# Two-layer block, layer 1's experts: weighted rows added to the outcome in DRAM by an indirect transfer

## The chip, the cores and the metric

One Trainium2 chip, one core of it. The metric is the device time of one execution in microseconds, the median of several runs. 512 tokens (two sequences) of 512 floats pass through two layers; all tensors are float32.

## The reference, cut to what is computed

Each of the two layers adds three parts to x: a cross-attention, a second mixing part (linear attention in layer 0, an mLSTM in layer 1) and a mixture of experts. The last one, layer 1's, is what the change touches:

```python
logits = xf @ gate_w + gate_b
scores = jax.nn.softmax(logits.astype(jnp.float32), axis=-1)
top_vals, top_idx = jax.lax.top_k(scores, TOPK)             # 2 of 16
cw = (jax.nn.one_hot(top_idx, N_EXPERTS) * weights[..., None]).sum(axis=1)
h = jnp.einsum('td,edh->teh', xf, w1) + b1                  # 512 -> 704
g = jnp.einsum('td,edh->teh', xf, w3) + b3
a = jax.nn.silu(h) * g
y = jnp.einsum('teh,ehd,te->td', a, w2, cw) + cw @ b2       # 704 -> 512
z = jax.nn.silu(xf @ sw1 + sb1) * (xf @ sw3 + sb3) @ sw2 + sb2
return (y + z).reshape(shape)
```

So the outcome is x plus the shared expert's z, plus for each token the rows that its two experts give, times their gates, plus the gates times b2.

## The kernel before, in words

The program is one stream per engine, written out stage by stage; engines meet at counting semaphores. x stays in SBUF as `x_tok`, 128 partitions by 4 tiles of tokens by 512. TensorE (PE) multiplies, VectorE (DVE) and ScalarE (ACT) take results out of PSUM, GpSimd (POOL) does some vector work and all indirect DMAs, SyncE (SP) issues the weight loads.

Both layers' experts share a class, `Experts`. Its steps, in the order of the work:

- `route_vector` takes softmax and the top experts per token. `place_tensor` (L1588) counts with triangular matmuls which place each token has in its expert's list, and `place_vector` (L1609 to L1631) works out from that the slot in the list (`slot`, 512 slots per expert), the place of a token's row in the experts' output (`first_at`, and `rest_at` for places from 128 on), the gate for either (`first_gate`, `rest_gate`), and whether any expert has over 128 tokens (`over`).
- `place_gpsimd` (L1643) scatters token numbers into a list in DRAM, one indirect DMA per tile of tokens and choice: 12 in layer 0, 8 in layer 1, 128 words each. The lists are cleared at the program's start (L878). `list_sync` (L1666) loads the list, `list_vector` casts it (L1673), `list_tensor` turns it (L1680), DVE copies it out again (L1675).
- `gather_rows` (L1686) fetches 128 token rows of 2 KB for an expert from `token_rows`, a copy of the normalized x in DRAM, in four buffers that rotate. `turn_rows` (L1714) transposes them, `rows_vector` (L1721) copies them out.
- Per expert of layer 1 PE makes 96 products with w1 and w3 (L242), turns the next expert's rows, and then makes the 18 products of the down projection of the expert before (L1757 to L1759, three per tile since w2 and the hidden rows are split in a high and a low part). ACT: six Silu (L2824), six casts of w2 (L1733), and the copy of the finished 128x512 bank to one of three buffers (L1766), which ACT then stores to `expert_out` in DRAM (L1768). The copy waits until the store before from the same buffer has landed.
- After the last expert POOL waits for all stores and gathers the rows back per tile of tokens and choice (L1795, 8 gathers in layer 1), DVE adds each, times its gate, to x (L1807), and SP stores a tile of x as soon as it is complete (L2868, `store_sync`, 4 stores of 256 KB).

The order around the change: in `experts1_sync` SP issues 48 weight loads of 1.4 MB, three per expert, into eight slots; load 8 waits for expert 0's up products, later ones for up or down products of an expert (L2629 on). In `experts1_vector` DVE adds the shared expert's three groups of products (L2745) and the bias products (L1660) to x before the first routed expert; the third group comes after the list. In `experts1_gpsimd` POOL adds `sb2` to x, scatters, issues three gathers, then the others as PE's turns free their buffers, and then the gathers back. A branch (`if_over`) holds a second form of the whole for experts with over 128 tokens; with these inputs it is not entered. At the start POOL makes the constants (L260 to L282) and SP, after its first loads, issues the clears of the two lists (L878).

Of the kernel before, what the change touches and what calls it, by code (L numbers as in the profile page):

```python
# [6 lines left out]
P = 128  # L7
F32 = mybir.dt.float32
F32R = mybir.dt.float32r
I32 = mybir.dt.int32  # L10
# [71 lines left out]
def build_program(nc, A, out_dram):  # L82
# [40 lines left out]
    HID0_AT, DOWN1_AT, HID1 = SPLIT_ARENA + 2 * SLOT, 11712, HT1 * P  # L123
# [13 lines left out]
    zero_words = sbuf("zero_words", [E0 * CHUNKS, P], I32)  # L137
    norm_small = sbuf("norm_small", [P, 2, NT, 10])
    square = sbuf("square", [P, DIM])

    token_rows = nc.dram_tensor("token_rows", (TOK, DIM), F32, kind="Internal").ap()
    ids, expert_out, expert_rest = {}, {}, {}
    for layer, n in ((0, E0), (1, E1)):
        ids[layer] = nc.dram_tensor(f"ids{layer}", (n * CAP, 1), I32, kind="Internal").ap()
        expert_out[layer] = nc.dram_tensor(f"expert_out{layer}", (n * P, DIM), F32, kind="Internal").ap()
        expert_rest[layer] = nc.dram_tensor(f"expert_rest{layer}", (n * (CAP - P), DIM), F32, kind="Internal").ap()
# [107 lines left out]
    IDENT, MASKS, TRI, NUMBERS, TOKEN_NO, ZERO_WORDS = 1, 2, 3, 4, 5, 6  # L254
# [4 lines left out]
    def constants_gpsimd(pool):  # L259
# [22 lines left out]
        pool.memset(zero_words[:, :], 0).then_inc(consts, 1)  # L282

# [581 lines left out]
    def cross0_sync(sp):  # L865
# [10 lines left out]
        sp.wait_ge(consts, ZERO_WORDS)  # L876
        for layer, n in ((0, E0), (1, E1)):
            sp.dma_start(ids[layer].rearrange("(c p) o -> c (p o)", p=P),  # L878
                         zero_words[0:n * CHUNKS, :]).then_inc(cleared[layer], 16)
# [601 lines left out]
    class Experts:  # L1481

        def __init__(self, layer, n, chosen, hidden_tiles, last_first, L, S, before=None):
# [10 lines left out]
            self.rank, self.is_first, self.base, self.at_f = (S(NT, chosen) for _ in range(4))  # L1494
            self.first_at, self.rest_at = (S(NT, chosen).bitcast(I32) for _ in range(2))
            self.first_gate, self.rest_gate = (S(NT, chosen) for _ in range(2))
# [3 lines left out]
            self.ids_row, self.ids = L(P), L(P)  # L1500
            self.gather = [arena[:, ARENA - (i + 1) * DIM:ARENA - i * DIM] for i in range(4)]

            self.totals = {"routed": 1, "shifted": 1, "exped": 1, "gates": 1, "ranked": 1, "slots": 2, "counted": 1,
# [5 lines left out]
                           "added": NT * chosen}  # L1509
# [4 lines left out]
            self.gathers, self.more_base = [0] * 4, [0] * 4  # L1514
            if before:
                for m in list(range(E0)) + [E0 + j % 8 for j in range(NT * TOP0) if j % 8 < 4]:
                    self.gathers[m % 4] += 16
                for j in range(NT * TOP0):
                    if j % 8 >= 4:
                        self.more_base[j % 8 - 4] += 16  # L1520
            self.stores = [16 * -(-(E0 - i) // 3) if before else 0 for i in range(3)]
# [76 lines left out]
        def place_vector(self, dve, rank_bank, count_bank):  # L1598
            n = self.n

# [4 lines left out]
            numbers, top3 = over_middle(expert_no[:, 0:n], NT), self.top[:, :, 0:self.chosen]  # L1605
# [7 lines left out]
            chosen = self.choice[:, :, 0:self.chosen]  # L1613
            own(dve.scalar_tensor_tensor(out=self.slot_f, in0=chosen, scalar=float(CAP), in1=self.rank, op0=ALU.mult,
                                         op1=ALU.add))
            dve.tensor_copy(self.slot, self.slot_f).then_inc(self.raised("slots"), 1)
            own(dve.tensor_scalar(self.is_first, self.rank, float(P), None, ALU.is_lt))
            own(dve.tensor_tensor(self.first_gate, self.is_first, top3, ALU.mult))
            dve.tensor_tensor(self.rest_gate, top3, self.first_gate, ALU.subtract)
            own(dve.tensor_scalar(self.base, self.rank, float(P - 1), None, ALU.min))  # L1620
            own(dve.scalar_tensor_tensor(out=self.at_f, in0=chosen, scalar=float(P), in1=self.base, op0=ALU.mult,
                                         op1=ALU.add))
            dve.tensor_copy(self.first_at, self.at_f)
            own(dve.tensor_scalar(self.base, self.rank, -float(P), 0.0, ALU.add, ALU.max))
            own(dve.scalar_tensor_tensor(out=self.at_f, in0=chosen, scalar=float(CAP - P), in1=self.base,
                                         op0=ALU.mult, op1=ALU.add))
            dve.tensor_copy(self.rest_at, self.at_f).then_inc(self.raised("slots"), 1)
# [9 lines left out]
        def place_gpsimd(self, pool):  # L1637
            self.wait(pool, "slots", 1)
            pool.wait_ge(consts, TOKEN_NO)
# [24 lines left out]
        def list_sync(self, sp):  # L1664
            self.wait(sp, "scattered", 16 * NT * self.chosen)
            sp.dma_start(self.ids_row.bitcast(I32)[0:self.n * CHUNKS, :],  # L1666
                         ids[self.layer].rearrange("(c p) o -> c (p o)", p=P)).then_inc(self.raised("ids_in"), 16)
# [1355 lines left out]
```

## Time and profile before

| | us |
|---|---|
| median of 3 runs | 1931.9 (1928.63 to 1932.24) |
| the profiled execution | 1931.5 |
| its span, first to last instruction | 1929.6 |
| PE busy in it | 1800.8 (93%) |
| DVE, ACT, POOL busy | 871.8, 675.7, 219.2 |
| mean granted TensorE clock | 0.972 of full speed |

Times in views of the trace are microseconds from the span's start. A group of instructions is named by line, engine and operation, then output<-input by the program's names; behind it the idle time of the engine in front of it and what ended that. "Issue" is time in which an engine waited for nothing that the profile shows. PEld is PE's weight load, which overlaps its products. The chain of waits is followed back from the last instruction, at each step to what released it.

### The profile page before, as it was taken

What the parts mean: (1) busy time and instruction counts of PE and PEld (TensorE: products, weight loads), DVE (VectorE), ACT (ScalarE), POOL (GpSimd) and SP (SyncE); (2) the same over time, 40 slices, a digit from 0 to 9 for tenths busy, and PEclk for the clock granted to TensorE, in tenths of its full rate; (3) what the DMA queues carried; (4) which work ended last, traced back from release to release, by engine and by line L of the source; (5) the groups of instructions that cost most, each with busy time, mean ns of one, the idle gap of its engine ahead of it and who ended that gap; (6) DMA issues with size and microseconds to landing.
All of it is one profiled execution on the core that took longest, in us unless ns stands there. A gap on an engine that the chain in (4) does not pass through costs nothing.

```text
span 1929.6 us, 27706 instructions
## 1 busy us (share of the span) xinstructions
PE 1800.8 (93%) x10942; PEld 1288.9 (67%) x10942; DVE 871.8 (45%) x1966; ACT 675.7 (35%) x1475; POOL 219.2 (11%) x309
## 2 busy tenths in 40 slices
PE   5999999999999999898999978999899899999995
PEld 3677777777646445456999845777545544699994
DVE  4243344333334665334666655555425411354454
ACT  2333333323203226313555635444415200233332
POOL 0000000000004042322111021101001101100001
PEclk9999999999999999899999999999899899899998
DMA  5011020111131011207999731112212400688882
GB/s 203 23 44 38 29 88 23 44 45 66 67 130 44 22 44 45 79 32 272 383 392 386 264 95 34 50 34 94 110 44 83 162 23 1 253 315 329 330 315 90
DMA packets 44831, 247.34 MB, mean 128 GB/s; under 512 B 5929, under 2 KB 6433, under 8 KB 21904
## 3 DMA queue, kind: packets, MB, share of 16 engines
q1 hardware_dynamic: 31776, 215.32, 29.4%
q0 software_dynamic: 6000, 17.58, 2.8%
q10 hardware_dynamic: 6912, 12.52, 1.7%
q8 instruction: 91, 1.49, 0.3%
q14 instruction: 52, 0.43, 0.1%
HBM read 229.83 MB, written 15.57 MB: 127 GB/s over the span
## 4 chain that ended last, share of the span: by engine, by line
PE 83%; DVE 6%; issue 6%; DMA 2%; POOL 2%; ACT 2%; POOLq 0%; DVEq 0%; ACTq 0%; SPq 0%
PE bank L586 26%; PE bank L242 26%; PE bank L248 8%; PE bank L728 3%; PE bank L756 3%; PE bank L1757 2%; PE bank L1759 2%; PE bank L1758 2%; PE bank L2656 2%; PE bank L682 2%; PE bank L675 2%; PE bank L1714 1%; POOL ids L1643 1%; DVE norm_small L307 1%; PE bank L1256 1%
## 5 line engine op out<-in xcount | busy, mean ns | idle before, releaser
L586 PE MATMUL bank<-split 128*128 128x512 f32 x2208 | 549.6, 401 | 24.0 <-DVE split L559 11.9
L586 PEld LDWEIGHTS bank<-split 128*128 128x128 f32 x2208 | 408.2, 190 | 154.4 <-issue 30.9
L242 PE MATMUL bank<-normed,weights 128*128 128x512 f32 (+1 forms) x592 | 248.6, 580 | 4.7 <-DVE normed L918 3.1
L242 PE MATMUL bank<-arena,weights 128*128 128x128 f32 (+1 forms) x1984 | 239.7, 280 | 3.7 <-issue 1.9
L242 PEld LDWEIGHTS bank<-arena,weights 128*128 128x128 f32 x1984 | 230.6, 192 | 15.0 <-issue 12.0
L242 PEld LDWEIGHTS bank<-normed,weights 128*128 128x128 f32 x592 | 114.4, 195 | 132.7 <-issue 124.9
L248 PE MATMUL bank<-weights,arena 128*128 128x512 f32 x288 | 133.5, 614 | 7.7 <-ACT arena L2534 5.8
L699 DVE TENSOR_REDUCE small<-bank 128x1 f32<-128x512 f32 x64 | 43.9, 686 | 155.6 <-PE bank L675 155.6
L618 DVE COPY arena<-bank 128x512 f32<-128x512 f32 x84 | 57.8, 689 | 117.2 <-PE bank L586 117.2
L736 ACT COPY normed<-bank 128x512 f32<-128x512 f32 x128 | 69.4, 591 | 109.1 <-PE bank L728 108.9
L248 PEld LDWEIGHTS bank<-weights,arena 128*128 128x128 f32 x288 | 54.8, 197 | 71.2 <-issue 62.9
L248 PE MATMUL bank<-weights,normed 128*128 128x512 f32 (+3 forms) x256 | 88.6, 493 | 7.9 <-ACT normed L420 6.8
L612 ACT COPY arena<-bank 128x512 f32<-128x512 f32 x76 | 44.2, 587 | 146.4 <-PE bank L586 114.6
L718 ACT ACTIVATE normed<-bank,small 128x512 f32<-128x512 f32 x64 | 44.2, 690 | 136.2 <-DVE small L701 136.0
L1686 POOL DMA_INDIRECT arena<-token_rows,arena x47 | 47.3, 1007 | 370.9 <-PE bank L1714 304.6
L2824 ACT ACTIVATE arena<-bank,cols 128x128 f32<-128x128 f32 x96 | 31.7, 365 | 150.8 <-PE bank L242 100.0
L2778 DVE SCALAR_TENSOR_TENSOR arena<-bank,cols,arena 128x128 f32<-128x128 f32 x96 | 30.5, 349 | 117.2 <-issue 67.1
L696 DVE CUSTOM_DVE_ANT_0 arena<-bank,arena 128x512 f32<-128x512 f32 x64 | 44.3, 692 | 83.9 <-PE bank L682 83.9
L1738 DVE TENSOR_TENSOR slot_r<-weights,normed_r 128x512 fp32r<-128x512 f32 x124 | 77.2, 685 | 1.0 <-ACT normed_r L1733 1.0
L559 DVE TENSOR_TENSOR split<-arena,split 128x512 fp32r<-128x512 f32 x92 | 59.9, 684 | 37.7 <-ACT split L554 37.6
L248 PEld LDWEIGHTS bank<-weights,normed 128*128 128x128 f32 x256 | 43.9, 209 | 43.1 <-issue 37.3
L1721 DVE COPY arena<-bank 128x512 f32<-128x512 f32 x47 | 32.5, 691 | 83.0 <-PE bank L1714 82.5
(314 smaller groups left out, 2426.7 us busy)
## 6 DMA issues: line engine op xcount, KB each, us to landing
weights<-in_L_ffn_re_w SPq DMA_DIRECT2D x62, 1024.0 KB, 8.6
weights<-in_L_w SPq DMA_DIRECT2D x20, 1408.0 KB, 12.3
arena<-in_ctxT SPq DMA_DIRECT2D x24, 1024.0 KB, 4.9
arena<-in_L_w SPq DMA_DIRECT2D x12, 1408.0 KB, 8.2
weights<-in_L_w_full SPq DMA_DIRECT2D x10, 1280.0 KB, 9.5
expert_out<-arena ACTq DMA_DIRECT2D x47, 256.0 KB, 8.4
weights<-in_L_ffn_sw SPq DMA_DIRECT2D x9, 1024.0 KB, 4.9
arena<-in_L_w_full SPq DMA_DIRECT2D x6, 1280.0 KB, 9.5
```

The source lines that it names most:

```text
L242: s = pe.matmul(out, w[:, k, j0:j0 + m], rhs(k), start=(k == 0), stop=(k == KT - 1))
L248: s = pe.matmul(out, lhs(k0 + k), w[:, k, j0:j0 + n], start=(start and k == 0), stop=(stop and k == KT - 1))
L559: dve.tensor_tensor(low, src, high, ALU.subtract).then_inc(self.low.sem, 1)
L586: s = pe.matmul(bank[:, :], still, moving, start=(n == 0), stop=(n == len(order) - 1))
L612: act.copy(dst, bank[:, :]).then_inc(self.kv_a.sem, 1)
L618: dve.tensor_copy(dst, self.kv_bank(c, g)[:, :]).then_inc(self.kv_v.sem, 1)
L696: dve.tensor_tensor_reduce(out=pr, in0=bank[:, :], in1=self.keep[c % 2], scale=1.0, scalar=-3.0e38, op0=ALU.add, op1=ALU.max, accum_out=st ...
L728: last = pe.transpose(banks[5 + s][:, t * P:(t + 1) * P], self.prob[s][:, t * P:(t + 1) * P], ident[:, :])
L736: act.copy(self.probT[s], blocks(banks[5 + s][:, :], CTX // P)).then_inc(self.probT_a.sem, 1)
L756: last = pe.matmul(banks[7][r:r + d, o:o + SEQ], self.v[c % 2][:, t, f:f + d], self.probT[s][:, t, i * SEQ:(i + 1) * SEQ], start=(t == 0), ...
L1686: pool.indirect_dma_start(out=self.gather[ex % 4], out_offset=None, in_=token_rows, in_offset=bass.IndirectOffsetOnAxis(ap=self.ids.bitcas ...
L1738: dve.tensor_tensor(w2.rounded[:, m, :], w2.view[:, m, :], self.w2_high[ex % 2][:, m, :], ALU.subtract).then_inc(self.raised("w2_low"), 1)
```

## The change

Layer 1's experts no longer store their rows to `expert_out`. x, with everything but the routed rows, is stored to the output in DRAM once, behind weight load 8. ACT takes a finished bank out with the token's gate as the scale of an ACTIVATE, and POOL adds these 128 rows to the output's rows by an indirect DMA that adds; each add waits for the one before to land. For that a list's slot holds the token's row number and its gate, 8 bytes; slots that no token fills point to 128 spare rows behind the 512 (`no_token`), which the output and `token_rows` now have. The spare rows are filled from x at the start of the linear attention. Rows of the output are now numbered p*4 + i, not i*128 + p. The gathers back, their additions on DVE, the four last stores, and for layer 1 the gates and places of `place_vector` are gone. The class is split in `Experts0`, with the old methods, and `Experts1`. The core of the diff:

```diff
 constants_gpsimd
+        pool.iota(token_row[:, :], pattern=[[1, NT]], base=0, channel_multiplier=NT)
+        pool.memset(no_token[:, :, 1], 0)
+        pool.iota(no_token[:, :, 0], pattern=[[1, P]], base=TOK, channel_multiplier=0).then_inc(consts, 1)
 linear_sync, behind its four weight loads
+        for rows_of in (token_rows, out_rows):
+            sp.dma_start(rows_of[TOK:ROWS_ALL, :], A["x"][:, 0, :]).then_inc(cleared[1], 16)
 place_gpsimd
-            pool.wait_ge(cleared[self.layer], 16)
+            pool.wait_ge(cleared[0], 16)
+            pool.wait_ge(cleared[1], 48)
...
-                        in_=token_no[:, i:i + 1], in_offset=None).then_inc(self.raised("scattered"), 16)
+                        in_=self.entry(i, k), in_offset=None).then_inc(self.raised("scattered"), 16)
+    class Experts1(Experts):
+        def entries_vector(self, dve):
+            dve.wait_ge(consts, NO_TOKEN)
+            for k in range(self.chosen):
+                dve.tensor_copy(self.entries.bitcast(I32)[:, :, k, 0], token_row[:, :])
+                dve.tensor_copy(self.entries[:, :, k, 1], self.top[:, :, k])
...
+        def list_vector(self, dve, bank):
+            n = self.n * CHUNKS
+            self.wait(dve, "ids_in", 16)
+            self.wait(dve, "bias_mm", NT)
+            dve.tensor_copy(self.b2[0:n, 0:P], self.ids_row.bitcast(I32)[0:n, :, 0])
+            dve.tensor_copy(self.b2[0:n, P:2 * P], self.ids_row[0:n, :, 1]).then_inc(self.raised("ids_f"), 1)
+            self.wait(dve, "ids_mm", 1)
+            dve.tensor_copy(self.id_of[:, 0:n], bank[:, 0:n])
+            dve.tensor_copy(self.gate_of[:, 0:n], bank[:, n:2 * n]).then_inc(self.raised("ids_v"), 1)
+        def list_tensor(self, pe, bank):
+            n = self.n * CHUNKS
+            self.wait(pe, "ids_f", 1)
+            pe.transpose(bank[:, 0:n], self.b2[0:n, 0:P], ident[0:n, 0:n])
+            pe.transpose(bank[:, n:2 * n], self.b2[0:n, P:2 * P], ident[0:n, 0:n]).then_inc(self.raised("ids_mm"), 1)
+        def gated(self, act, out, bank, chunk):
+            return act.activation(out, bank[:, :], ACT.Identity, scale=self.gate_of[:, chunk:chunk + 1])
+        def add_rows(self, pool, rows_in, chunk):
+            return pool.indirect_dma_start(
+                out=out_rows, out_offset=bass.IndirectOffsetOnAxis(ap=self.id_of[:, chunk:chunk + 1], axis=0),
+                in_=rows_in, in_offset=None, compute_op=ALU.add)
+        def out_scalar(self, act, ex):
+            if ex == 0:
+                self.wait(act, "ids_v", 1)
+            if ex >= 3:
+                act.wait_ge(rows_added, 16 * (ex - 2))
+            self.wait(act, "down_mm", ex + 1)
+            self.gated(act, self.out[ex % 3], banks[6 + ex % 2], ex * CHUNKS).then_inc(self.raised("out_a"), 1)
+        def out_gpsimd(self, pool, ex):
+            if ex == 0:
+                pool.wait_ge(x_stored, 16)
+            else:
+                pool.wait_ge(rows_added, 16 * ex)
+            self.wait(pool, "out_a", ex + 1)
+            self.add_rows(pool, self.out[ex % 3], ex * CHUNKS).then_inc(rows_added, 16)
 experts1_sync, in the loop of the weight loads
             load_expert(sp, n)
+            if n == 8:
+                sp.wait_ge(sh1_add, 3 * NT)
+                sp.dma_start(out_rows[0:TOK, :].rearrange("(p i) d -> p i d", p=P), x[:, :, :]).then_inc(x_stored, 16)
 experts1_vector
-        for i in range(NT):
-            moe1.combine_vector(dve, i)
 experts1_gpsimd
-        for ex in range(3, E1):
-            moe1.gather_rows(pool, ex)
+        moe1.gather_rows(pool, 3)
+        for ex in range(E1):
+            if ex + 4 < E1:
+                moe1.gather_rows(pool, ex + 4)
+            if ex:
+                moe1.out_gpsimd(pool, ex - 1)
+        moe1.out_gpsimd(pool, E1 - 1)
         moe1.if_over(pool, moe1.rest_gpsimd)
-        moe1.combine_gpsimd(pool)
 at the end, on SP
-        for i in range(NT):
-            moe1.wait(sp, "added", TOP1 * (i + 1))
-            sp.dma_start(out_dram[:, i, :], x[:, i, :]).then_inc(stored, 16)
-        sp.wait_ge(stored, 16 * NT)
+        sp.wait_ge(x_stored, 16)
+        sp.wait_ge(rows_added, 16 * E1)
```

## Rows read from the trace of the kernel before

**Rows 1.** the page: busy time (share of the span) and the chain by engine

```profile
PE 1800.8 (93%) x10942; PEld 1288.9 (67%) x10942; DVE 871.8 (45%) x1966; ACT 675.7 (35%) x1475; POOL 219.2 (11%) x309
...
PE 83%; DVE 6%; issue 6%; DMA 2%; POOL 2%; ACT 2%; POOLq 0%; DVEq 0%; ACTq 0%; SPq 0%
```

**Rows 2.** table by stage: length, busy of PE, PEld, DVE, ACT, POOL, clock, DMA share, GB/s

```profile
1689.03:1704.31 15.28, 15.28 (x120) 14.53 (x120) 7.77 (x16) 5.79 (x13) 0.95 (x1) 1.00 0.84 327
1887.75:1903.25 15.50, 15.50 (x119) 14.67 (x118) 9.22 (x18) 6.27 (x14) 0.00 (x0) 1.00 0.05 19
1903.25:1929.60 26.35, 3.39 (x15) 2.46 (x14) 6.01 (x8) 0.59 (x1) 8.44 (x8) 0.66 0.45 141
```

**Rows 3.** the chain in order of time, the tail: start us, us, what

```profile
1907.35 3.57 DMA expert_out<-arena
...
1910.95 0.70 issue
...
1919.72 5.33 DMA arena<-expert_out,small
```

**Rows 4.** instructions on x_tok from 1900 on: the stores of x

```profile
L2868 SPq DMA_DIRECT2D out_x<-x_tok x4: 332/338/352, 1917.2 to 1926.8; - x4
...
DMA to landing us min/median/max: 2.4/3.0/3.8
```

**Rows 5.** DMA of 1903 to 1930; issues of 1911 to 1912; of 1906 to 1909

```profile
q0 software_dynamic: 640, 2.10, 27.0%
...
arena<-expert_out,small POOLq DMA_INDIRECT x1, 3.4
...
expert_out<-arena ACTq DMA_DIRECT2D x1, 256.0 KB, 3.6
```

**Rows 6.** DMA issues, us to landing: first scatter of layer 1's lists, last

```profile
ids<-token_no,small POOLq DMA_INDIRECT x1, 3.4
...
ids<-token_no,small POOLq DMA_INDIRECT x2, 10.0
```

**Rows 7.** DMA issues of 1857.18 to 1872.46, beside weight loads

```profile
expert_out<-arena ACTq DMA_DIRECT2D x1, 256.0 KB, 8.4
```

**Rows 8.** timeline of the tail: start us, us, engine, line, operation [idle before]

```profile
1902.66 0.59 ACT L1766 COPY arena<-bank 128x512 f32<-128x512 f32 x1 [5.18 <-PE bank L1759]
...
1903.27 0.33 ACTq L1768 DMA_DIRECT2D expert_out<-arena  x1
...
1906.74 0.59 ACT L1766 COPY arena<-bank 128x512 f32<-128x512 f32 x1 [3.49 <-PE bank L1759]
...
1911.65 0.96 POOL L1795 DMA_INDIRECT arena<-expert_out,small  x1 [87.95 <-DMA expert_out<-arena]
...
1921.27 0.96 POOL L1795 DMA_INDIRECT arena<-expert_out,small  x1 [0.30 <-issue]
```

**Rows 9.** groups by line, whole span: bank copies and activations on ACT

```profile
L1766 ACT COPY arena<-bank 128x512 f32<-128x512 f32 x47 | 27.6, 587 | 43.6 <-PE bank L1759 42.2
...
L610 ACT ACTIVATE arena<-bank,cols 128x512 f32<-128x512 f32 x32 | 22.0, 687 | 46.6 <-PE bank L586 35.6 <-PE bank L242 11.0
```

**Rows 10.** timeline of the list of layer 1 and what follows

```profile
1642.55 0.21 DVE L1673 CAST arena<-arena 64x128 f32<-64x128 int32 x1
...
1642.90 0.34 PE L1680 MATMUL bank<-ident,arena 64*128 64x64 f32 x1 [1.00 <-DVE arena L1673]
...
1643.78 0.98 POOL L1686 DMA_INDIRECT arena<-token_rows,arena  x1 [44.82 <-DVE arena L1675]
...
1657.90 0.63 PE L1714 MATMUL bank<-ident,arena 128*128 128x128 f32 x4 [1.33 <-DVE arena L2765]
```

**Rows 11.** timeline of DVE before the scatters of layer 1

```profile
1586.36 0.23 DVE L1609 TENSOR_TENSOR small<-expert_no,small 128x64 f32<-128x64 f32 x1 [1.39 <-PE bank L1588]
```

**Rows 12.** DMA issues of 1671 to 1676, behind the eighth weight load

```profile
arena<-in_L_w SPq DMA_DIRECT2D x1, 1408.0 KB, 15.3
```

**Rows 13.** timeline of SP at the start: the clears of the lists

```profile
13.48 0.96 SPq L878 DMA_DIRECT2D ids<-zero_words  x2
```

More of the change, by code:

```diff
@@ L1508, in __init__ @@
                            "w2_high": n * hidden_tiles, "w2_low": n * hidden_tiles, "hid_high": n, "hid_low": n, "down_mm": n, "out_a": n,
[L1509 removed]
+                           "added": NT * chosen * (1 - layer)}
             base = before.totals if before else dict.fromkeys(self.totals, 0)
@@ L1760, in down_tensor @@
             s.then_inc(self.raised("down_mm"), 1)
-        def out_scalar(self, act, ex):
-            if ex >= 3:
-                act.wait_ge(out_stored[ex % 3], self.stores[ex % 3] + 16 * (ex // 3))
-            self.wait(act, "down_mm", ex + 1)
-            act.copy(self.out[ex % 3], banks[6 + ex % 2][:, :]).then_inc(self.raised("out_a"), 1)
-            self.wait(act, "out_a", ex + 1)
-            act.dma_start(expert_out[self.layer][ex * P:(ex + 1) * P, :], self.out[ex % 3]).then_inc(out_stored[ex % 3], 16)
-        def wait_stored(self, e):
-            for i in range(3):
-                e.wait_ge(out_stored[i], self.stores[i] + 16 * -(-(self.n - i) // 3))
-        def back_buffer(self, j):
-            b, turn = j % 8, j // 8
-            if b < 4:
-                g = (self.n + b) % 4
-                return self.gather[g], gather_in[g], self.gathers[g] + 16 * ((self.n + b) // 4 + 1 + turn)
-            return self.more[b - 4], more_in[b - 4], self.more_base[b - 4] + 16 * (turn + 1)
-        def combine_gpsimd(self, pool):
-            self.wait(pool, "slots", 2)
-            self.wait_stored(pool)
-            for j in range(NT * self.chosen):
-                i, k = divmod(j, self.chosen)
-                buf, landed, _ = self.back_buffer(j)
-                if j == 0:
-                    self.wait(pool, "tok_mm", self.n)
-                if j >= 8:
-                    self.wait(pool, "added", j - 7)
-                pool.indirect_dma_start(
-                    out=buf, out_offset=None, in_=expert_out[self.layer],
-                    in_offset=bass.IndirectOffsetOnAxis(ap=self.first_at[:, i, k:k + 1], axis=0)).then_inc(landed, 16)
-        def combine_vector(self, dve, i):
-            for k in range(self.chosen):
-                j = i * self.chosen + k
-                buf, landed, value = self.back_buffer(j)
-                dve.wait_ge(landed, value)
-                if k:
-                    self.wait(dve, "added", j)
-                dve.scalar_tensor_tensor(out=x[:, i, :], in0=buf, scalar=self.first_gate[:, i, k:k + 1],
-                                         in1=x[:, i, :], op0=ALU.mult, op1=ALU.add).then_inc(self.raised("added"), 1)
-            self.wait(dve, "added", self.chosen * (i + 1))
         def rest_semaphores(self):
@@ L1990, in build_program @@
     moe0.rest_layout(REST_L)
-    moe0.run_layout(RUN_L, [x1.qT[:, m, :] for m in range(KT)])
+    moe0.run_layout(RUN_L)
+    moe0.more = [x1.qT[:, m, :] for m in range(KT)]
     assert REST_L.at <= SPLIT_ARENA and RUN_L.at <= SPLIT_ARENA + 4 * DIM + KT * CTX
```

330 lines of the change are left out of this document (209 added, 121 removed).

## The prediction, made before the changed kernel was run

> **What bounds the kernel now.** The page's first part shows TensorE (PE) busy for 93% of the span, and the chain of waits puts 83% of it on PE; DVE and ACT stay under half [rows 1]. So a part of the change counts only where it delays PE, or after PE has ended. The table by stage comes next: one expert of layer 1 takes 15.28 us with PE busy all of it, ACT 5.79, DVE 7.77 and a DMA share of 0.84, while the last 26.35 us hold only 3.39 us of PE [rows 2]. This tail is what the change rewrites. The chain in order of time shows it as one line of waits: a store of 3.57, 0.70 until POOL moves, eight gathers, and 5.33 until the seventh has landed behind its issue [rows 3]; two additions follow, and the last store of x, issued at 1926.8, lands in 2.4, at 1929.2 [rows 4]. The span ends 0.4 later.
>
> The profiled execution took 1931.5 us and its span 1929.6, so 1.9 lie around the span. The median of the runs is 1931.9, 0.4 over that execution; I work out a difference of the span and take it from the median. About 0.2% (4 us) is what a measurement can tell from no change.
>
> **The tail, step by step.** Removed: the wait for the store, 8 gathers, 8 additions and 4 stores of x, all after 1907.35. In their place expert 15's rows are added in DRAM behind expert 14's, since each add waits until the one before has landed. Call T the time from POOL's issue of an add to its landing. The trace has no add in DRAM, so T is bounded:
> - Lower end 3.4: the tail's first gather, the same 128 rows of 2 KB, queues idle [rows 5].
> - Upper end 10.0: the last of the lists' eight scatters, which queue up behind one another (the first took 3.4) [rows 6]; a plain store beside weight loads is near it with 8.4 [rows 7].
> - Taken, 5.1: an add writes 256 KB to DRAM, as the idle store does in 3.6 [rows 5]; POOL issues it in 0.96 where ACT needs 0.33 (+0.6) [rows 8]; and it must also read its destination: the eight gathers kept the 16 engines busy for 27.0% of 26.6 us, 0.9 each [rows 5], so +0.9. The idle rows are the nearest, since the weight loads are over: the DMA share is 0.05 from 1887.75 to 1903.25 [rows 2].
>
> Copy 14 out of PSUM starts at 1902.66 [rows 8]. With a gate as its scale it is an ACTIVATE of a bank, 0.69, no longer a COPY of 0.59 [rows 9]: it ends at 1903.35. POOL starts 0.3 later, the gap in front of its other indirect DMAs [rows 8]: 1903.65. Landing 1908.75. Copy 15 ends at 1906.74 + 0.69 = 1907.43 [rows 8], so the add before is the later. From a landing to POOL's next issue it is 0.70 [rows 3]: 1909.45, landing 1914.55, end of the span 0.4 later: 1914.95. In general the end is 1904.75 + 2T while T is over 3.4. Saved: 1929.6 − 1914.95 = 14.65.
>
> By the Trainium skill (DMA: Bandwidth & Descriptors, Anatomy of one DMA) a DMA issued by GpSimd costs about 2.0 us plus its bytes at 436 GB/s; for 256 KB that is an estimate of 2.6, with a second read 3.2, and by it the tail would end near 1911.5. This case's trace has 3.4 for a gather of that size from its issue [rows 5], so measured rows stand in the sum.
>
> **The list.** DVE casts the list once (0.21) and PE turns it once (0.34), and PE waits for both before the last shared products [rows 10]. Now two casts stand in front and two turns follow: +0.2 and +0.2, 0.4 on PE's path. Bounds: 0.1, if the second of each is pipelined, and 0.9, if stepping over pairs slows the casts. The second copy behind the turns delays the gathers that start at 1643.78 by 0.2, hidden: PE wants their first rows at 1657.90 [rows 10].
>
> **Costed at nothing, with the cover of each.**
> - Four small copies that form the entries: DVE idles 1.39 us before its step of 0.23 at 1586.36, waiting for PE [rows 11]. Four of at most 0.23 are 0.9, and that is their price uncovered. Nine small operations behind it go, on a DVE that waits for PE; nothing gained.
> - Entries of 8 bytes: still 128 rows per scatter. The scatters follow 1586.36 within some 12 us and land in 10.0 at most, so by about 1609; the list is cast at 1642.55 [rows 6, 10, 11]. Some 30 us of cover.
> - 1 MB of x stored behind the ninth weight load, on SP's queue. Its sum is ready by then. It holds up the loads behind it by 0.4 of issue and by 1 MB; those land in up to 15.3 after about 1673, so at 1688, and the expert that needs them starts at 1704.31 [rows 2, 12]: 16 us of cover. It must itself land before add 0, about 1690.
> - ACT: 0.1 more per copy, in 9.5 us of idle per expert [rows 2].
> - POOL's queue: add ex−1 stands behind the gather for ex+4 and in front of the one for ex+5. The copy comes some 4 us after the turn that releases that gather, so nothing is held up while an add lands within 15.3, and a gather is wanted three experts later.
> - DMA engines: 16% of 15.28 are idle, 2.4 us per expert [rows 2]. A store of 256 KB goes, a read and a write of 256 KB come: 0.9 more.
> - Start: three more small POOL instructions, while SP reaches the clears only at 13.48 [rows 13]; uncovered, 0.6. The two fills of 256 KB stand behind the loads for the linear attention, and POOL needs them before layer 0's scatters, hundreds of us later.
>
> Sum: −14.65 + 0.4 = −14.25, and 1931.9 − 14.25 = 1917.65, so 1917.7. The case spans T = 3.4 (copy 15 leads: 1907.43 + 0.3 + 3.4 + 0.4 = 1911.5, −17.7 with the list: 1914.2) to T = 10.0 (1924.75, −4.45: 1927.4).
>
> **Rivals.**
> 1. *Adds that go row by row.* If a row's read and write don't overlap the next row's, T is long on idle queues too. For: the scatters' landing grew from 3.4 to 10.0 over eight issued 1.3 apart, so each took 1.3 + 6.6/7 = 2.2 us for 8 tiny rows per engine [rows 6]. Against: gathers of 2 KB rows land 0.9 of engine time each [rows 5]. Were it 2.2 for every 512 bytes of a row, T = 4 × 2.2 + 2.2 = 11.0: end 1926.75, with the list −2.45: 1929.5. The Trainium skill (Collectives: The Full Stack, The bandwidth ceiling) states that an add in the DMA engine needs two source reads on one ring and so runs at about half of a copy's rate; no row here shows an add.
> 2. *Adds that don't fit into an expert's time, the slower side.* Beside weight loads a store takes 8.4 [rows 7]; an add whose two legs each queue so takes 17.4, with the 0.7 an 18.1 over 15.28. Add 0 starts at about 1690, the loads have ended by 1887.75: 10.9 adds by then, the other 5.1 at 5.8, end 1917. No loss yet. At 22 per add, add 9 lands at 1910, and expert 12's copy, which reuses its buffer and was due at 1902.66 − 2 × 15.28 = 1872, waits for it; PE and the last loads slip by 38, 10.7 adds land by 1925, and 5.3 follow at 5.8: end 1956, 1958 from the median, 26 slower. It decides from about 20 us per add.
> 3. *Gate and Silu need different tables.* Then ACT loads tables twice per expert, hidden in its idle time but for the tail, where one load stands before copy 14. The attention's 32 Identity activations of a bank stand at 0.69 with no load in the group [rows 9], but Silu beside Identity isn't shown. Priced by the 0.69 + 0.59 of two such instructions, about 1.3: 1919.0.
>
> **Chances.** Forecast 0.78; rival 1 0.08, half of it within 0.2%; rival 2 0.08; rival 3 0.06. Faster 0.88, same 0.04, slower 0.08. Low 1913.9: T = 3.4 and the list at 0.1. High 1927.4: T = 10.0. That holds the forecast and rival 3 and leaves out the two others.
>
> **What would show it.** At the end two adds, the first issued near 1904 and the second T + 0.7 later; no vector work behind PE's last product; an expert still 15.28 with PE full; PE's gap and turns before the last shared products longer by 0.4. I am wrong if adds are issued more than 15.3 apart in mid-stage, if PE waits there for weights or copies, if ACT loads tables among the experts, or if T on idle queues is over 10.

## The result, and the profile after

| | before | after |
|---|---|---|
| median of the runs made together, us | 1930.27 (4 runs, 1927.54 to 1932.24) | 1916.70 (4 runs, 1914.78 to 1917.79) |
| ratio, 95% interval | | 0.993 (0.9912 to 0.9947) |
| span of the profiled execution | 1929.6 | 1916.0 (the execution took 1917.79) |
| start of copy 14 (expert 14's rows out of PSUM) | 1902.66 | 1902.90 |
| from there to the end of the span | 26.94 | 13.10 |

The change makes the kernel 13.6 us faster, between 10 and 17 by the interval; forecast were 14.2, with 1917.7 as the time. Run 8 below is the same kernel measured again beside more runs of the kernel before, and gives 12.9. Lines have moved: L242 is now L248 (products with w1 and w3), L1766 is L2060 (ACT's copy, now with the gate), and POOL's add is L2063.

The first part of the page, and its chain by engine, beside [rows 1]:

```profile
PE 1798.6 (94%) x10943; PEld 1288.2 (67%) x10943; DVE 865.6 (45%) x1955; ACT 677.2 (35%) x1475; POOL 247.4 (13%) x320
...
PE 85%; DVE 6%; issue 4%; DMA 2%; ACT 2%; POOL 1%; POOLq 0%; DVEq 0%; ACTq 0%; SPq 0%
```

PE's busy time is the same within 2.2 us and its share has risen: time in which PE had nothing to do is gone. The timeline of ACT and of POOL in the tail, which stands where [rows 3, 8] stood:

```profile
1902.90 0.69 ACT L2060 ACTIVATE arena<-bank,arena 128x512 f32<-128x512 f32 x1 [5.19 <-PE bank L1733]
1906.98 0.69 ACT L2060 ACTIVATE arena<-bank,arena 128x512 f32<-128x512 f32 x1 [3.39 <-PE bank L1733]
...
1889.53 5.68 POOL L2063 DMA_INDIRECT out_x<-arena  x1 [13.22 <-ACT arena L2060]
1904.35 1.55 POOL L2063 DMA_INDIRECT out_x<-arena  x1 [9.14 <-ACT arena L2060]
1909.74 1.55 POOL L2063 DMA_INDIRECT out_x<-arena  x1 [3.84 <-DMA out_x<-arena]
```

Copy 14 ends at 1903.59, add 14 starts 0.76 later and lands in 5.1 (1909.45); add 15 starts 0.29 after that landing, though its own copy ended at 1907.67, and lands in 4.8 (1914.54); the span ends 1.46 later (1.47 by the finer times of the packed trace). There is no vector work and no store behind PE's last product. The issue with its landing, and SP's waits in the last stretch, where the first column of numbers is the wait in us:

```profile
out_x<-arena POOLq DMA_INDIRECT x2, 5.0
...
SPq L3008 <- DMA out_x<-arena: 38.3, 1, 38.3
SPq L3064 <- PEq L3064: 1.2, 1, 1.2
```

SP waits for the adds and then 1.2 in the join of the engines (L3064). Before, the same two waits were 2.0 for the store and 0.2 for the join.

One expert in mid-stage, and the stretch of twelve experts (length, busy PE, PEld, DVE, ACT, POOL, clock, DMA share, GB/s):

```profile
1857.00:1872.30 15.30, 15.30 (x119) 14.53 (x118) 7.74 (x16) 5.91 (x13) 2.04 (x1) 1.00 0.85 308
1704.55:1887.99 183.44, 183.44 (x1418) 174.42 (x1418) 92.75 (x181) 70.78 (x156) 33.44 (x21) 1.00 0.87 315
```

PE is still full [rows 2], and twelve experts take 183.44, as they did before (1704.31 to 1887.75). The same stretch of before:

```profile
1704.31:1887.75 183.44, 183.44 (x1419) 174.42 (x1418) 92.70 (x181) 69.52 (x156) 7.65 (x8) 1.00 0.81 314
```

The list, beside [rows 10]:

```profile
1642.63 0.21 DVE L2047 CAST arena<-arena 64x128 f32<-64x128 int32 x1
1642.76 0.21 DVE L2048 COPY arena<-arena 64x128 f32<-64x128 f32 x1
1643.12 0.34 PE L2056 MATMUL bank<-ident,arena 64*128 64x64 f32 x1 [1.14 <-DVE arena L2048]
1643.25 0.31 PE L2057 MATMUL bank<-ident,arena 64*128 64x64 f32 x1
1643.49 1.22 PE L2795 MATMUL bank<-weights,arena 128*128 128x512 f32 x1
```

From the first cast to the first product it is 0.86; it was 0.62. The second cast starts 0.13 behind the first and the second turn 0.13 behind the first: each is partly hidden in the one before, which is why they cost 0.24 and not 0.4.

### The profile page after: what moved, and what is told of

It is laid out like the page before. It is cut to its first block, busy times and chain, and to the rows that moved or that the text cites. A ratio compares the mean times of both kernels' runs of the same rounds, so it can differ in the third digit from the quotient of the medians.

```text
span 1916.0 us, 27701 instructions
## 1 busy us (share of the span) xinstructions
PE 1798.6 (94%) x10943; PEld 1288.2 (67%) x10943; DVE 865.6 (45%) x1955; ACT 677.2 (35%) x1475; POOL 247.4 (13%) x320
## 4 chain that ended last, share of the span: by engine, by line
PE 85%; DVE 6%; issue 4%; DMA 2%; ACT 2%; POOL 1%; POOLq 0%; DVEq 0%; ACTq 0%; SPq 0%
PE bank L248 28%; PE bank L595 26%; PE bank L254 8%; PE bank L737 3%; PE bank L765 3%; PE bank L1731 3%; PE bank L1733 3%; PE bank L1732 2%; PE bank L2795 2%; PE bank L684 2%; PE bank L691 2%; PE bank L1688 1%; POOL ids L1642 1%; DVE norm_small L316 1%; PE bank L1268 1%
## 5 line engine op out<-in xcount | busy, mean ns | idle before, releaser
L248 PE MATMUL bank<-normed,weights 128*128 128x512 f32 (+1 forms) x592 | 246.9, 577 | 4.7 <-DVE normed L927 3.1
L248 PE MATMUL bank<-arena,weights 128*128 128x128 f32 (+1 forms) x1984 | 241.8, 282 | 3.0 <-DVE arena L1695 1.8
L248 PEld LDWEIGHTS bank<-arena,weights 128*128 128x128 f32 x1984 | 232.7, 193 | 14.4 <-issue 11.4
L248 PEld LDWEIGHTS bank<-normed,weights 128*128 128x128 f32 x592 | 113.2, 193 | 132.2 <-issue 124.9
L627 DVE COPY arena<-bank 128x512 f32<-128x512 f32 x84 | 57.9, 689 | 117.1 <-PE bank L595 117.1
```

The source lines that it names most:

```text
L248: s = pe.matmul(out, w[:, k, j0:j0 + m], rhs(k), start=(k == 0), stop=(k == KT - 1))
L627: dve.tensor_copy(dst, self.kv_bank(c, g)[:, :]).then_inc(self.kv_v.sem, 1)
```

## The experiments

My theory was the prediction's: the tail is two adds in a row, each T long, and the list costs PE a little; mid-stage hides the rest. Open were: what T is made of, whether the chain of waits between adds is what binds, how far mid-stage is from binding (rival 2), and two gaps that I had wrong, 0.76 and 1.46. Runs 1 to 6 and 9 to 11 were executed once each, so their times alone show little. The executions differ by up to 10 us ahead of the experts (copy 14 starts between 1901.16 and 1910.95 in them), so all tails are counted from the start of copy 14; after the change that is 13.10. Tails differ by themselves too: in runs 4, 5, 9 and 11, whose edits take nothing out of the tail, they are 12.5 to 13.0, since the two adds landed in 4.5 to 5.0.

**1. A scatter that doesn't add.** It leaves the addition out: the rows overwrite.

```diff
-                in_=rows_in, in_offset=None, compute_op=ALU.add)
+                in_=rows_in, in_offset=None)
```

> The 16 transfers of expert rows write without adding (left out: the addition itself, so the output holds single experts' rows). My sum made T of the copy of 3.6, POOL's issue of 0.6 and 0.9 for the second read. If the second read costs 0.9, each of the two last transfers lands in about 4.1 instead of 5.1 and 4.8, POOL's instruction falls from 1.55 to about 0.97 us, and the tail behind copy 14 is about 1.8 us shorter. Rival (adds are serialized row by row inside an engine): T falls by far more than 1 us, to 3. Beside weight loads: if the second read queues like the first, 10 us falls to about 8.4, as the plain store had; if it costs only its bytes, to about 9.

Measured 1923.01 us, the tail 10.35. POOL's timeline at the end:

```profile
1897.60 5.08 POOL L2063 DMA_INDIRECT out_x<-arena  x1 [13.82 <-ACT arena L2060]
1912.41 0.97 POOL L2063 DMA_INDIRECT out_x<-arena  x1 [9.74 <-ACT arena L2060]
1916.49 0.97 POOL L2063 DMA_INDIRECT out_x<-arena  x1 [3.10 <-ACT arena L2060]
```

The last two landed in 2.7 and 3.3 from issue:

```profile
DMA to landing us min/median/max: 2.7/3.0/3.3
```

Without the addition it is 3.0 from issue to landing, with it 5.0: the addition costs 2.0, of which 0.58 are POOL's (1.55 against 0.97). My theory had 4.1 for this run, and the 3.0 is what the rival had given, adds whose rows are serialized inside an engine. So T came out as forecast from two terms that were both off. The load on the DMA engines says the same. These are packets, MB and share of 16 engines of POOL's queue from 1903 to 1917, for two plain scatters here (experts 13 and 14) and for the last two adds after the change:

```profile
q0 software_dynamic: 160, 0.52, 9.8%
...
q0 software_dynamic: 288, 0.52, 30.0%
```

The windows are 14 and 13 us long, so a scatter takes all 16 engines for 0.7 us and an add for 2.0. The addition costs 1.3 of engine time, more than a second pass of the same rows would. How a row's read, sum and write lie in time inside an engine, no run shows. In mid-stage the scatter lands in 8.5 and the add in 9.5, and the DMA share of twelve experts is 0.81 here and 0.87 with the addition.

**2. Two chains.** Odd experts' rows go into a second tensor, so that an add waits for the one two before. This leaves them out of the result.

```diff
-                pool.wait_ge(rows_added, 16 * ex)
...
+                pool.wait_ge(rows_added[ex % 2], ROWS_BASE[ex % 2] + 16 * (ex // 2))
...
+            self.add_rows(pool, self.out[ex % 3], ex * CHUNKS, (out_rows, second_rows)[ex % 2]).then_inc(rows_added[ex % 2], 16)
```

> Odd experts add to a second tensor in DRAM and wait only for the odd add before (left out of the output: the odd experts' rows). The last add then waits for its own copy only. Theory: it starts 0.8 us after copy 15 ends, at about 1908.4 instead of 1909.74, so the chaining of the last two costs 1.3 us and the span ends that much earlier; T of the last is still 5. Rival: the two adds in flight together slow each other, and nothing is gained.

Measured 1916.82, the tail 11.65:

```profile
1904.90 1.55 POOL L2067 DMA_INDIRECT out_x<-arena  x1 [9.14 <-ACT arena L2064]
1908.96 1.55 POOL L2067 DMA_INDIRECT second_rows<-arena  x1 [2.50 <-ACT arena L2064]
```

Add 15 now waits for ACT and starts 0.74 behind its copy, 5.51 after the start of copy 14 where it was 6.84: 1.33 are gone, and that is what the order between the last two adds costs. The other 0.12 of the 1.45 lie in the last add's landing. Add 14 lands in 4.7, 0.6 after add 15 was issued, so the rival, adds that slow each other, was tested for little more than that overlap.

**3. Every add twice**, the second time into a spare tensor and behind the landing of the first; the next expert's add and the buffers of ACT's copies wait for the second one. The result is complete; the work of the adds is doubled, to reach the point from which rival 2 decides.

```diff
             self.add_rows(pool, self.out[ex % 3], ex * CHUNKS).then_inc(rows_added, 16)
+            pool.wait_ge(rows_added, 16 * (ex + 1))
+            self.add_rows(pool, self.out[ex % 3], ex * CHUNKS, second_rows).then_inc(again, 16)
```

> Each expert's rows are added twice, the second time to a spare tensor, one behind the other, and the third next buffer waits for both. Nothing is left out. This is the prediction's slower rival by force: 10.3 + 0.6 twice is 21 to 22 us per expert beside weight loads, over 15.3. Theory: a backlog of 5 to 6 us per expert, ACT's copies wait for their buffer from about expert 7 on, PE gets gaps, the loads spread out; the last four experts go at 11.2 each. Span 1960 to 2000, of which the tail alone explains 11. Rival (only the tail counts, the middle hides it): span 1926 to 1928.

Measured 1947.87, the tail 38.6. Both expectations missed. POOL's timeline in mid-stage and in the tail:

```profile
1695.47 2.10 POOL L2067 DMA_INDIRECT out_x<-arena  x1 [17.14 <-ACT arena L2064]
1706.20 1.95 POOL L2067 DMA_INDIRECT second_rows<-arena  x1 [8.64 <-DMA out_x<-arena]
1711.58 1.58 POOL L2067 DMA_INDIRECT out_x<-arena  x1 [1.80 <-DMA second_rows<-arena]
1722.99 2.03 POOL L2067 DMA_INDIRECT second_rows<-arena  x1 [9.84 <-DMA out_x<-arena]
...
1891.68 2.08 POOL L2067 DMA_INDIRECT out_x<-arena  x1 [3.90 <-DMA second_rows<-arena]
...
1939.26 1.55 POOL L2067 DMA_INDIRECT second_rows<-arena  x1 [3.53 <-DMA out_x<-arena]
```

The stretch of twelve experts:

```profile
1705.00:1888.40 183.40, 183.40 (x1417) 174.38 (x1417) 92.77 (x180) 70.71 (x157) 47.13 (x31) 1.00 0.98 335
```

The first line is expert 0's first add, the line of 1891.68 expert 11's: 196.2 us for eleven pairs, so two adds take 17.8 us per expert, against 15.29. Single ones vary much: the add of 1706.20 has landed by 1711.58, the next only shortly before 1722.99. In those 5.1 us all queues together moved 224 GB/s, in the 11.1 us behind them 361. That fits adds that go fast where the weight loads leave room; nothing here moved the loads to try it. PE is full throughout, with a DMA share of 0.98. The first add of expert 11 is issued 29 us behind its copy. It was close: copy 13 found its buffer free by 1.2 us (the second add of expert 10 was issued at 1886.23 and landed in 5.2, the copy starts at 1892.66). Copy 15, behind PE's last product, did wait for its buffer: ACT idled 5.8 in front of it, against 3.4 after the change. The rest of the backlog comes out in the tail, where the adds are issued 4.9 to 6.0 apart. The bottom line for rival 2: at 17.8 us per expert PE still loses nothing, and the loss is one of the tail. The 20 us from which rival 2 was to decide were not reached, so that bound is untested.

**4. The low halves of the last w2 later on DVE.** They are worked out behind expert 15's fourth hidden tile, no longer directly behind expert 14's.

```diff
-            if ex == E1 - 2:
-                moe1.w2_vector(dve, E1 - 1, expert_weights[3 * E1 - 1])
...
+                if ex == E1 - 1 and m == 4:
+                    moe1.w2_vector(dve, E1 - 1, expert_weights[3 * E1 - 1])
```

> DVE makes the low parts of the last expert's w2 (six operations on two SBUF operands, 3.7 us) after its fourth hidden tile instead of right behind those of expert 14. In the changed kernel add 13 took POOL 5.68 us instead of 2.06 and landed in 14.1 with idle queues, while these six ran. If DVE's operations hold up POOL's work on the descriptors, add 13 falls to about 1.6 us on POOL and lands in about 5, and add 14 stays at 1.55 as DVE is done by then. The span does not change (within 1 us), since add 13 had landed 0.7 us before add 14 was issued. Rival (it is the DMA queues, or ACT's casts, which stay where they are): add 13 stays near 5.7 and 14.

The 14.1 given there for add 13 is the landing of the store of x; add 13 landed in 8.8 after the change. DVE's timeline after the change beside add 13, which POOL starts at 1889.53 and for which it needs 5.68:

```profile
1886.48 3.69 DVE L1712 TENSOR_TENSOR long_slot_r<-weights,normed_long_r 128x512 fp32r<-128x512 f32 x6
1890.09 3.69 DVE L1712 TENSOR_TENSOR long_slot_r<-weights,w_long_r 128x512 fp32r<-128x512 f32 x6
```

And POOL in this run:

```profile
1889.56 2.06 POOL L2063 DMA_INDIRECT out_x<-arena  x1 [13.22 <-ACT arena L2060]
```

The edit moves the six of 1890.09 and leaves those of 1886.48, while ACT's casts stay where they were. Add 13 takes POOL 2.06 and lands in 5.2. So DVE's subtractions of two operands in SBUF hold up POOL while it makes ready an indirect transfer: they ran beside add 13 for 4.2 us and now do for 0.6, and over the 1.55 of an add with an idle DVE it took 4.1 and now takes 0.5. The Trainium skill (SBUF — State Buffer, Who interferes with whom) says that a DVE operation with two SBUF inputs contends with a GpSimd operation that reads SBUF, but infers that it doesn't stall a DMA's descriptors; here it did, by 3.6 us. The time, 1917.62, does not move: add 13 has 15 us.

**5. One turn.** It leaves out the gates (all 0.5): one cast and one turn.

```diff
-            dve.tensor_copy(self.b2[0:n, P:2 * P], self.ids_row[0:n, :, 1]).then_inc(self.raised("ids_f"), 1)
...
-            pe.transpose(bank[:, n:2 * n], self.b2[0:n, P:2 * P], ident[0:n, 0:n]).then_inc(self.raised("ids_mm"), 1)
```

> This run leaves out the gates (each row's gate is 0.5): the list is cast once and turned once before the last shared products, as in the kernel before. If the second cast and the second turn are what the list costs PE, the time from the list's cast to the first shared product behind the turns falls by 0.24 us, back to 0.62, and the tail from copy 14 stays at 13.1. The step of my prediction had 0.4 here; its bounds were 0.1 and 0.9. A rival: the 0.24 comes from casts that step over pairs of 4 bytes, not from the second of each; then the single cast would still show more than 0.21.

Measured 1915.76. The cast starts at 1641.00, the first product at 1641.62: 0.62, as before the change, and the tail is 12.74, shorter since add 14 landed in 4.8. The one cast that is left still steps over pairs of words and takes 0.21, as long as before the change, so the stepping costs nothing.

```profile
1641.00 0.21 DVE L2047 CAST arena<-arena 64x128 f32<-64x128 int32 x1
1641.62 2.93 PE L2793 MATMUL bank<-weights,arena 128*128 128x512 f32 x3
```

**6. The branch first.** POOL loads the overflow's value and branches ahead of the last two adds.

```diff
-        moe1.out_gpsimd(pool, E1 - 1)
-        moe1.if_over(pool, moe1.rest_gpsimd)
...
+        moe1.if_over(pool, last_and_rest, last)
```

> POOL loads the value for the overflow branch and branches before adds 14 and 15, and both arms of the branch then issue the two adds. Theory: the 1.46 us from the last landing to the end of the span hold POOL's load, its branch and the join of the engines, which no longer stand behind add 15; the gap falls to about 0.5 as in the kernel before, and the tail from copy 14's start from 13.10 to about 12.1. Rival: the gap belongs to the landing of an indirect transfer itself, and stays at 1.5. If POOL's branch were slow to fetch its instructions, add 14 would instead start later, by up to some us.

Measured 1916.09, the tail 12.54. Add 15 was issued at 1908.12 and landed in 4.8, at 1912.88; the span ends at 1914.35, 1.47 later, and SP's wait in the join stays 1.2. My theory fell; the 0.56 that the tail is shorter lie in add 14, which landed in 4.6 and not 5.1.

**7. Expert 14's down products in the middle of expert 15's up products**, with edit 6. Expert 15's hidden rows are split in high and low parts in two halves, so that PE has products to make behind its last up products, and ACT takes copy 14 out in the middle too.

```diff
+                if ex == E1 - 1 and n == 0:
+                    moe1.down_tensor(pe, ex - 1, expert_weights[3 * ex - 1])
...
+                if ex == E1 - 1 and m == 4:
+                    moe1.w2_vector(dve, E1 - 1, expert_weights[3 * E1 - 1])
+                    moe1.hidden_part(dve, ex, 0, 4, 1)
```

> Two edits on top of the change. The branch goes ahead of adds 14 and 15 as in the run before; and in the last expert, expert 14's down products are moved to the middle of expert 15's up products, so that copy 14 is done about 3.5 us earlier and add 14 can land before copy 15 is ready. Theory: add 14 is issued near 1901 and lands near 1906, add 15 waits for its own copy alone (0.76 after it, near 1908.4) and not for a landing (1909.74 after the change), 1.3 us less; with the 1.0 of the branch the time falls by 2.3 against the changed kernel, to about 1914.4. Rival: the moved products open a gap in PE, since DVE must deliver the first half of expert 15's hidden rows at once, and the gain of 1.3 is paid back on PE; then copy 15 ends that much later.

**8. The changed kernel again.**

> The changed kernel again, unedited, on the same chip as the run before it, to be compared with it: 1916.7, within 1.5 either way; the tail from copy 14's start 13.1, with 1.5 from the last landing to the end of the span.

Run 7 took 1919.85 (6 runs, 1914.96 to 1921.59), run 8 took 1918.65 (6 runs, 1915.11 to 1924.40); against the kernel before both stand at 0.993 (0.9916 to 0.9952 and 0.9916 to 0.9954). They can't be told apart. Run 8 is 0.45 above the 1916.7 ± 1.5 that was expected of it, and 12.9 below the 1931.51 that the kernel before took in the 11 runs beside it. A row of run 7's chain at the start of an expert, and then the timeline of ACT and POOL at its end:

```profile
1693.63 10.72 PE bank L248 x96
```

```profile
1903.70 0.69 ACT L2072 ACTIVATE arena<-bank,arena 128x512 f32<-128x512 f32 x1 [3.28 <-PE bank L1743]
1911.37 0.69 ACT L2072 ACTIVATE arena<-bank,arena 128x512 f32<-128x512 f32 x1 [5.18 <-PE bank L1743]
...
1905.17 1.72 POOL L2075 DMA_INDIRECT out_x<-arena  x1 [9.20 <-ACT arena L2072]
1912.82 1.55 POOL L2075 DMA_INDIRECT out_x<-arena  x1 [5.93 <-ACT arena L2072]
```

In run 8 the same chain row is at 1693.15, copy 14 at 1906.78, copy 15 at 1910.86 and add 15 at 1913.48. Counted from the chain row, copy 14 comes 3.6 earlier in run 7, copy 15 at the same time (217.74 and 217.71, so no gap opened in PE), and add 15 1.1 earlier (219.19 and 220.33), released by ACT and no longer by a landing. This step did what it should. Then add 15 landed in 5.4 where it took 4.8 in run 8, and the end comes 0.6 earlier (226.07 and 226.65); the branch gave nothing. Half a microsecond is under what these runs can show.

**9. Copies 14 and 15 on DVE.**

```diff
+            dve.tensor_scalar(self.out[ex % 3], banks[6 + ex % 2][:, :], self.gate_of[:, ex * CHUNKS:ex * CHUNKS + 1],
+                              None, ALU.mult).then_inc(self.raised("out_a"), 1)
...
+        moe1.out_vector(dve, E1 - 2)
+        moe1.out_vector(dve, E1 - 1)
```

> Copies 14 and 15 out of PSUM, with their gates, are made by DVE instead of ACT; nothing else changes. After the change, POOL's add started 0.76 us after ACT's copy ended, where the step of my prediction took 0.3 from gaps behind landings. Theory: the 0.76 belongs to a copy whose data must be written before POOL is told, and to ACT; behind a DVE operation POOL starts within about 0.4 of its end. Rival: it belongs to POOL, which wakes after 9 us of rest, and stays 0.76 whichever engine made the copy. The last add waits for the landing of the one before in either case, so the tail gets at most 0.4 shorter, by add 14.

Measured 1919.07, the tail 12.84:

```profile
1904.46 0.75 DVE L2079 TENSOR_SCALAR arena<-bank,arena 128x512 f32<-128x512 f32 x1 [2.17 <-PE bank L1733]
...
1905.97 1.55 POOL L2063 DMA_INDIRECT out_x<-arena  x1 [9.60 <-DVE arena L2079]
```

The copy ends at 1905.21 and POOL starts 0.76 later, as behind ACT. The rival held: the 0.76 is not the copying engine's. Run 2 had 0.74 after a rest of 2.5, so the length of POOL's rest does not set it either. What sets it stands in the packed trace, among POOL's waits, which the views leave out. In front of add 14 POOL has a wait for the copy as an instruction of its own, which ends at 1903.64; the add starts 0.71 behind it. The wait for the landing before is part of the DMA instruction itself, and add 15, which it releases, starts 0.27 behind the landing. The kernel before shows both with the releasers exchanged: its first gather back stands behind a separate wait for a landing, which ends at 1910.95, and starts 0.70 later; its gathers of token rows hold their wait for PE's turns themselves and start 0.26 behind the turns' semaphore, as this one, raised at 1684.94:

```profile
1685.20 0.95 POOL L1686 DMA_INDIRECT arena<-token_rows,arena  x1 [11.67 <-PE bank L1714]
```

So the gap goes with the kind of wait and not with what is waited for. It is 0.69 to 0.80 behind a separate wait in every add that such a wait releases, in all traces. No run changed which wait stands apart.

**10. A store behind the last add**, 256 KB into spare DRAM.

```diff
         sp.wait_ge(rows_added, 16 * E1)
+        sp.dma_start(spare_rows, x[:, 0, :]).then_inc(cleared[1], 16)
         sp.wait_ge(cleared[0], 16)
-        sp.wait_ge(cleared[1], 48)
+        sp.wait_ge(cleared[1], 64)
```

> Behind the landing of the last add, SP stores 256 KB of x into a spare piece of DRAM and waits for it. The span gets about 3.6 us longer. It is here for the 1.46 us from the last landing to the end of the span. Rival A: the 1.46 belongs to the landing of an indirect transfer, or to POOL, whose ring must be empty before the engines join; then it passes beside the store, and the span ends 0.4 after the store's landing, as in the kernel before. Rival B: it belongs to the join after a tail in which the other engines have rested, and the span still ends 1.5 after the store's landing.

Measured 1920.37. SP's waits:

```profile
SPq L3007 <- DMA out_x<-arena: 37.3, 1, 37.3
SPq L3010 <- DMA spare_rows<-x_tok: 1.7, 1, 1.7
SPq L3066 <- PEq L3066: 0.2, 1, 0.2
```

The store is issued at 1916.13 and lands in 2.0, where I had assumed 3.6; the span ends 0.5 after it, at 1918.6, and the wait in the join is back at 0.2. From add 15's landing (1916.04) to the end it is 2.6, so the store costs 1.1 and hides the rest. Rival A held: the extra 1.0 runs out beside a store.

**11. SP waits for each add in turn.**

```diff
-        sp.wait_ge(rows_added, 16 * E1)
+        for ex in range(1, E1 + 1):
+            sp.wait_ge(rows_added, 16 * ex)
```

> SP waits for each of the sixteen adds in turn instead of once for the last, so that it has not rested for 38 us when the last lands. If SP's rest is behind the 1.46 us from the last landing to the end of the span, it falls towards 0.4; in the trace of before SP moved within 0.1 after a rest of 41.8, so I expect it to stay 1.46.

Measured 1917.99. Add 15 was issued at 1910.26, landed in 4.5, and the span ends 1.47 after that. SP's rest is not the cause. So the last 1.47 follow the landing of an indirect transfer, whichever branch, kind of transfer (run 1 has 1.47 too) or rest of SP stands there. The packed trace has the instruction that takes them, a DRAIN of POOL's in the join of the engines (L3064 after the change). It starts at 1910.55, behind POOL's branch, and ends at 1915.81, 1.23 behind the landing; the span ends 0.24 behind it. In run 10 it ends at 1917.27, also 1.23 behind add 15's landing, and the store lands only at 1918.12. In the kernel before it was over at 1926.67, 0.9 behind the last gather's landing and ahead of the last store's at 1929.20. It ends 1.23 or 1.24 behind the last indirect landing in all traces with the change but run 3's, where it is 1.89 and the end 2.13 behind. Why the drain takes 1.2 beyond the landing, and more in run 3, no run shows.

## Why the prediction was right

**Right in its path; its sizes agree in part by luck.** The sum of the tail was 14.65 less and 13.84 were measured; the four terms that differ make up the 0.81. Without their signs they are 2.23, so errors that cancel brought the sum this near:

| step of the prediction | forecast | measured | effect on the end |
|---|---|---|---|
| POOL starts behind copy 14 | 0.3 | 0.76 | +0.46 |
| T, first and second add | 5.1, 5.1 | 5.1, 4.8 | −0.30 |
| landing to POOL's next issue | 0.70 | 0.29 | −0.41 |
| landing to the end of the span | 0.4 | 1.46 | +1.06 |

The largest miss is the last. The 0.4 came from [rows 3, 4], where the last transfer was a plain store issued by SP; the last transfer now is an indirect one of POOL's, the join waits for POOL's DRAIN behind it, and run 10 shows that a store behind it hides this. The two gaps in front of the adds, 0.3 and 0.70, were the right pair in the wrong places: 0.70 was a gather behind a wait instruction of its own, which is add 14's case, and it is 0.27 where the DMA instruction waits itself, which is add 15's. Exchanged they cancel but for 0.05.

**T was right by two errors.** I built it from an idle store of 3.6, 0.6 of issue and 0.9 of a second read. Run 1 gives 3.0 for the plain scatter, its issue included, and 2.0 for the addition. Both builds give 5.0 or 5.1. Had I split T so, the lower bound of 3.4 would have been out of reach: in the eleven traces with an addition the last two adds land in 4.5 to 5.4. For the load in mid-stage the 0.9 was right: the DMA share of twelve experts went from 0.81 to 0.87, 0.06 x 15.29 = 0.9 us each. In the tail the addition's part is 1.3, 2.0 for the add against 0.7 for the scatter (run 1). The Trainium skill (Collectives: The Full Stack, The bandwidth ceiling) has an add run at about half a copy's rate, since it reads two sources; here an add takes nearly three times the engine time of the plain scatter, and 5.0 against 3.0 in latency. Rival 1 with its 11.0 is ruled out. A weaker form of it, rows serialized in an engine at a lower price each, is not: run 1's 3.0 was its figure.

**The list**: 0.24, inside its bounds of 0.1 and 0.9; run 5 shows that the second cast and the second turn are all of it. Copy 14 starts 0.24 later in the profiled pair, but with up to 10 us between runs ahead of it, that alone would prove little.

**Rival 2** is ruled out for this kernel, and its price was wrong too: I had 17.4 for an add beside loads, both legs at 8.4 each. After the change:

```profile
DMA to landing us min/median/max: 4.8/9.5/10.4
```

9.5 is little more than the plain store's 8.4 [rows 7] and the plain scatter's 8.5 (run 1). Adding up two latencies was this rival's failed step: beside weight loads the addition costs 1.0. Run 3 shows besides that an add's time is not one number: its adds beside the loads landed in 5.1 to 12.1.

**Rival 3**: no table load stands among the experts, and the ACTIVATE with a gate takes 0.69.

**Costed at nothing.** ACT has 0.12 more per expert (5.91), as forecast. The 1 MB of x was issued at 1672.98 and landed in 14.1, at 1687.1; add 0 starts at 1690.89, a margin of 3.8, narrow but kept. One sentence was wrong: that nothing on POOL's queue is held up.

```profile
1690.89 2.12 POOL L2063 DMA_INDIRECT out_x<-arena  x1 [17.12 <-ACT arena L2060]
1693.32 0.98 POOL L1667 DMA_INDIRECT arena<-token_rows,arena  x1 [0.30 <-issue]
```

The turns that free this gather's buffer ended at 1685.2, and before the change the gather was issued at 1685.20. Now it stands behind add 0, which starts at 1690.89, behind copy 0; the gather comes 8 us later, as do those after it. I had the order right and also that the copy comes some 4 us after that turn, but drew the wrong conclusion: an add that waits for a later copy holds the gather behind it by just that, and by its own gap and 2.1 of issue. It is harmless, since the rows are wanted experts later, which was the cover I had named. The start of the program, with its three more small instructions on POOL, was not tried by itself.

## What to carry to other kernels

A chain of store, gather and add behind the last product is worth replacing by an add in DRAM, if the part beside the other work has room: here 15.29 us per expert against adds of 9.5; two per expert take 17.8, and their backlog has to come out behind the last product. What stays at the end is one add's latency for each add that must wait for another, 5 us; letting the last but one finish early removed its wait (run 7), but the 0.6 us gained can't be told from the spread of the runs. Take each small gap from a row of the same make: the gap at the end from one with the same kind of transfer on the same queue, and the gap in front of a DMA from one that waits in the same way, in an instruction of its own or in the DMA's. Three of the four errors here were gaps borrowed from another kind.

## What the runs showed of the hardware

- An indirect add of 128 rows of 2 KB to DRAM takes 4.5 to 5.4 us from issue to landing on idle queues and 9.5 beside weight loads; the same scatter without the addition takes 3.0 and 8.5. POOL is busy for 1.55 and 0.97 of it. On idle queues the add keeps the 16 DMA engines busy for 2.0 us and the scatter for 0.7.
- POOL's work for an indirect DMA is held up by DVE operations with two operands in SBUF: 5.68 where they ran beside it for 4.2 us, 2.06 where they did for 0.6, 1.55 with none; for the plain scatter 5.08 against 1.46.
- The execution ends 1.47 us after the last landing if that is an indirect transfer of POOL's (2.13 in run 3), since POOL's DRAIN in the join ends 1.23 behind it, and 0.4 to 0.5 if a plain store of SP's comes last.
- An indirect DMA of POOL's starts 0.70 to 0.80 behind a wait that is an instruction of its own, and 0.26 or 0.27 behind what releases it if the DMA instruction holds the wait, be that an engine's result or a landing.
